# GNN and FFN layer on one core: tile 0 in float32, row statistics by ScalarE, counts placed along the products

## What is computed

```python
h = gat_layer(layernorm(x), W1, att_src1, att_dst1, b1, src, dst, heads=8, out_ch=128, concat=True)
h = relu(h)
x = x + gat_layer(h, W2, att_src2, att_dst2, b2, src, dst, heads=1, out_ch=768, concat=True)
x = x + ffn(layernorm(x)[None])[0]
# in a gat_layer: h = x @ W.T; logits a_src[src] + a_dst[dst], leaky_relu 0.2,
# softmax over the edges of one dst, out = sum of alpha * h[src]
```

## Time and profile before

| | us |
|---|---|
| median of 3 runs (lowest, highest) | 758.25 (758.07, 758.85) |
| profiled execution, its own time | 758.19 |
| its span, first to last instruction | 756.4 |
| PE busy in the span | 719.8 (95%) |
| DVE, ACT, POOL busy | 541.2, 370.2, 77.4 |

### The profile page before, as it was taken

How to read it: one execution, slowest core, us unless ns; L and a number is a source line. 1 busy time by engine, 2 the same in 40 slices (tenths; PEclk the granted TensorE clock), 3 DMA queues, 4 the chain that set the end, 5 groups by cost and what they waited for, 6 DMA issues and landing times.

```text
span 756.4 us, 12941 instructions
## 1 busy us (share of the span) xinstructions
PE 719.8 (95%) x4567; PEld 658.0 (87%) x4567; DVE 541.2 (72%) x983; ACT 370.2 (49%) x698; POOL 77.4 (10%) x94
## 2 busy tenths in 40 slices
PE   1879999988999999999999999999999999999988
PEld 1769999867899999999999999999988898888965
...
GB/s 298 132 89 174 156 188 152 168 180 282 97 46 57 102 34 69 34 68 47 54 200 0 1 55 0 1 0 34 220 278 76 179 106 165 90 70 168 21 27 56
DMA packets 39772, 78.97 MB, mean 104 GB/s; under 512 B 4057, under 2 KB 25500, under 8 KB 38829
## 3 DMA queue, kind: packets, MB, share of 16 engines
q1 hardware_dynamic: 34057, 60.60, 26.6%
...
## 4 chain that ended last, share of the span: by engine, by line
PE 88%; DVE 6%; ACT 3%; issue 2%; DVEq 1%; POOL 0%; DMA 0%; SPq 0%; ACTq 0%; POOLq 0%
PE bank L1104 22%; PE bank L1244 13%; PE bank L1085 12%; PE bank L1173 11%; PE bank L1017 11%; PE bank L1319 5%; PE bank L1339 4%; PE bank L943 2%; PE bank L1225 1%; PE bank L1120 1%; DVE y L1826 1%; PE bank L958 1%; PE bank L1291 1%; ACT w_hi L706 1%; PE bank L1307 1%
## 5 line engine op out<-in xcount | busy, mean ns | idle before, releaser
L1104 PE MATMUL bank<-PT,h1s 125*128 125x250 f32 x800 | 175.8, 374 | 0.0
L1104 PEld LDWEIGHTS bank<-PT,h1s 125*128 125x128 f32 x800 | 148.6, 190 | 15.6
L1658 DVE SCALAR_TENSOR_TENSOR L<-asb,nadh 125x1250 f32<-125x1250 f32 x80 | 118.0, 1517 | 6.7 <-PE bank L1085 4.8
L747 ACT COPY PT<-bank 125x500 f32<-125x500 f32 x200 | 100.1, 596 | 40.1 <-PE bank L1085 40.1
L1666 DVE CUSTOM_DVE_ANT_0 L<-L,LC 125x1250 f32<-125x1250 f32 x80 | 113.4, 1456 | 0.0
L734 ACT ACTIVATE L<-L,nm 125x1250 f32<-125x1250 f32 x80 | 107.7, 1370 | 2.1 <-DVE nm L1670 2.1
L1085 PEld LDWEIGHTS bank<-ident,L 125*125 125x125 f32 x800 | 95.4, 192 | 7.6 <-ACT L L734 4.8
L1085 PE MATMUL bank<-ident,L 125*125 125x125 f32 x800 | 96.5, 277 | 4.9 <-ACT L L734 4.6
L1836 DVE TENSOR_TENSOR x2f<-bank,x2f 125x384 f32<-125x384 f32 x20 | 10.3, 551 | 58.6 <-PE bank L1339 58.6
L1503 DVE TENSOR_TENSOR hotr<-iota,r 125x1500 f16<-125x1500 f16 x50 | 46.8, 935 | 3.1 <-issue 3.1
L1017 PE MATMUL bank<-w_hi,xT_hi 128*125 128x352 f32 (+2 forms) x168 | 37.1, 371 | 8.2 <-ACT w_hi L706 4.1
...
## 6 DMA issues: line engine op xcount, KB each, us to landing
...
```

Of the source, the lines that this page charges most:

```text
L747: act.copy(PT[(k - lag) % 2][:, 2 * b:2 * b + 2, :], bank[TBANK[b]][0:NP, 0:2 * GW].rearrange("p (s n) -> p s n", s=2)).then_inc(tb_evac, 1)
L1104: mm = pe.matmul(bank[2 + (k - lag) % 2][:, 0:GW], h1s[q][:, s, :], PT[(k - lag) % 2][:, s, :], start=(s == 0), stop=(s == NT - 1))
L1658: dve.scalar_tensor_tensor(L[r][:, :], asb[q][0:NP, 1, :], nadh[q][:, t:t + 1], asb[q][0:NP, 0, :], ALU.add, ALU.max).then_inc(stt_done, 1)
```

## The change

Tile 0 is multiplied in float32 by 18 matmuls straight from w1_sb (first_products), as soon as W1 comes, now in three transfers instead of two; its logits come from six small matmuls with watt1 (first_columns, read by DVE in first_column_out). Tile 1 takes over tile 0's former place. For tiles 2 to 9 ACT sums the rows and the squared differences with its accumulator (sums, squares) and POOL makes mean, variance, rstd and offset of them. ACT copies the 16 logit columns (cols) in features_out, in place of DVE's asc. Counts 2, 3, 4, 6, 7 and 8 stand between pieces of the products, 1 after tile 1's, 5 ahead of tile 5's, 9 ahead of turn(9). Products wait for each bank's copy (h1_piece) instead of all. 46 transposes of the identity, whose result is not used, stand ahead of and between PE's first steps. statistics(0) comes earlier on DVE, the ACT table load ahead of the loads of W1.

```diff
+            def scale_by_sums(t):
+                p = t % 2
+                pool.wait_ge(sum_ready, t - 1)
+                pool.tensor_scalar(stats[p][:, 0, 0:1], mv[p][:, 0:1], -1.0 / D, None, ALU.mult).then_inc(mean_ready, 1)
+                pool.wait_ge(sq_ready, t - 1)
+                pool.tensor_scalar(var[p][:, :], mv[p][:, 1:2], 1.0 / D, LN_EPS, ALU.mult, ALU.add).then_inc(rstd_ready, 1)
+                pool.wait_ge(rstd_ready, 2 * t - 1)
+                pool.wait_ge(xn_ready, t - 1)
+                pool.tensor_tensor(rstd[p][:, :], var[p][:, :], powers[:, 0:1], ALU.pow).then_inc(rstd_ready, 1)
+                pool.wait_ge(rstd_ready, 2 * t)
+                pool.wait_ge(mean_ready, t - 1)
+                pool.tensor_scalar(nmr[p][:, :], stats[p][:, 0, 0:1], rstd[p][:, 0:1], None, ALU.mult).then_inc(nmr_ready, 1)
             pool.wait_ge(powers_set, 2)
-            for t in range(NT):
-                scale_of(t)
+            scale_of(0)
+            scale_of(1)
+            for t in range(2, NT):
+                scale_by_sums(t)
...
-            for k in range(0, KD, 3):
-                act.dma_start(w1_sb[:, k:k + 3, 0:HC], W1T.rearrange("(k p) n -> p k n", p=128)[:, k:k + 3, :]
-                              ).then_inc(w1_in[k // 3], 16)
+            for k in range(0, KD, 2):
+                act.dma_start(w1_sb[:, k:k + 2, 0:HC], W1T.rearrange("(k p) n -> p k n", p=128)[:, k:k + 2, :]
+                              ).then_inc(w1_in[k // 2], 16)
...
-                for b, c0, c1 in (THIRDS if t < FUSED else HALVES):
+                pieces = THIRDS if t < FUSED else HALVES
+                for b, c0, c1 in pieces:
                     c1 = min(c1, HC)
                     c = act.copy(h1st[t % 2][:, c0:c1], bank[b][0:NP, 0:c1 - c0])
+                    if c0 != pieces[-1][1]:
+                        c.then_inc(h1_piece, 1)
+                if 0 < t < FUSED:
+                    freed(act, rows_full, t - 1)
+                    freed(act, col_done, t - 1)
+                    c = act.copy(cols[t % 2][:, :], bank[5][0:NP, LOGIT0:LOGIT0 + 2 * H])
                 c.then_inc(h1_out, 1)
+            def sums(t):
+                act.wait_ge(x_in[t % 2], TWO * (t // 2 + 1))
+                act.wait_ge(xt_full, t - 1)
+                act.activation(xn[t % 2][:, :], xin[t % 2][:, :], ACT.Identity, bias=0.0, scale=1.0,
+                               accum_out=mv[t % 2][:, 0:1]).then_inc(sum_ready, 1)
+            def squares(t):
+                act.wait_ge(mean_ready, t - 1)
+                act.activation(xn[t % 2][:, :], xin[t % 2][:, :], ACT.Square, bias=stats[t % 2][:, 0, 0:1], scale=1.0,
+                               accum_out=mv[t % 2][:, 1:2]).then_inc(sq_ready, 1)
...
-            rows_turned(0)
+            first_turned()
             for k in range(KD):
-                if k % 3 == 0:
-                    act.wait_ge(w1_in[k // 3], 16)
+                act.wait_ge(w1_in[k // 2], 16)
                 act.copy(w1_hi[:, k, 0:HC], w1_sb[:, k, 0:HC]).then_inc(w1_hi_done, 1)
             normalise(1)
+            sums(2)
+            squares(2)
+            features_out(0)
             rows_turned(1)
             log_counts(0)
             normalise(2)
-            log_counts(1)
-            features_out(0)
+            store_h1(0)
             load_x(4)
-            for i in range(1, NT):
-                if i > 1:
-                    features_out(i - 1)
-                    if i + 3 < NT:
-                        load_x(i + 3)
-                if i + 1 < NT:
-                    log_counts(i + 1)
-                store_h1(i - 1)
+            sums(3)
+            rows_turned(2)
+            squares(3)
+            normalise(3)
+            for i in range(2, NT):
+                features_out(i - 1)
+                if i in (2, 5, 8):
+                    log_counts({2: 1, 5: 5, 8: 9}[i])
                 if i + 1 < NT:
                     rows_turned(i + 1)
+                if i in (4, 7):
+                    log_counts({4: 4, 7: 8}[i])
+                if i + 3 < NT:
+                    load_x(i + 3)
                 if i + 2 < NT:
+                    sums(i + 2)
+                store_h1(i - 1)
+                if i + 2 < NT:
+                    squares(i + 2)
                     normalise(i + 2)
+                if i in (2, 3, 5, 6):
+                    log_counts({2: 2, 3: 3, 5: 6, 6: 7}[i])
...
+            def keep_busy(count):
+                for _ in range(count):
+                    pe.transpose(bank[3][:, 0:128], ident[:, :], ident[:, :])
             def spans_turned():
                 pe.wait_ge(consts_made, 2)
+                keep_busy(26)
                 pe.wait_ge(span_step, 6)
                 pe.transpose(bank[2][0:2 * NW, 0:NS], vv[:, :], ident[0:NS, 0:NS]).then_inc(span_turned, 1)
+                keep_busy(8)
                 pe.wait_ge(span_step, 7)
                 pe.transpose(bank[2][0:1, 128:128 + 2 * NW], vm[:, :], ident[0:2 * NW, 0:2 * NW]
...
+                        if part == 0 and b == 6:
+                            pe.wait_ge(h1_piece, 2 * t - 1)
+                        elif part == 0 and b == 7 and t < NT - 1:
+                            pe.wait_ge(h1_piece, 2 * t)
+                        elif part == 0:
+                            pe.wait_ge(h1_out, t)
                         for k in range(KD):
-                            if t == 0 and b == 6 and part < 2:
+                            if t == 1 and b == 6 and part < 2:
                                 pe.wait_ge((w1_hi_done, w1_lo_done)[part], k + 1)
...
+                        if count and (part, b) == count[0]:
+                            count_edges(count[1])
...
+            def first_products():
+                pe.wait_ge(xT_ready, 1)
+                for k in range(KD):
+                    pe.wait_ge(w1_in[k // 2], 16)
+                    for b, c0, c1 in THIRDS:
+                        c1 = min(c1, HC)
+                        mm = pe.matmul(bank[b][0:NP, 0:c1 - c0], xT_first[:, k, :], w1_sb[:, k, c0:c1],
+                                       start=(k == 0), stop=(k == KD - 1))
+                    mm.then_inc(w1_used if k < KD - 1 else h1_full, 1)
+            def first_columns():
+                pe.wait_ge(watt_done, 3)
+                for k in range(KD):
+                    mm = pe.matmul(bank[5][0:NP, LOGIT0:LOGIT0 + 2 * H], xT_first[:, k, :], watt1[:, k, :],
+                                   start=(k == 0), stop=(k == KD - 1))
+                mm.then_inc(first_logits, 1)
             spans_turned()
+            keep_busy(12)
             turn(0)
-            pe.wait_ge(xT_ready, 1)
-            products(0, parts=(0,), pieces=THIRDS[:2])
+            first_products()
+            turn(1)
             pe.wait_ge(consts_made, 14)
             pe.wait_ge(plan_ready, 1)
             count_edges(0)
-            turn(1)
-            products(0, parts=(1, 2), pieces=THIRDS[:2])
             pe.wait_ge(w1n_in, 16)
             pe.wait_ge(attz_set, 3)
+            pe.wait_ge(h1_out, 1)
...
-            count_edges(1)
+            products(1, parts=(0,), pieces=THIRDS[:2])
             pe.wait_ge(watt_done, 1)
...
-            pe.wait_ge(watt_done, 3)
-            products(0, pieces=THIRDS[2:])
-            count_edges(2)
-            for i in range(1, NT):
+            products(1, parts=(1,), pieces=THIRDS[:2])
+            first_columns()
+            turn(2)
+            products(1, parts=(2,), pieces=THIRDS[:2])
+            products(1, pieces=THIRDS[2:])
+            count_edges(1)
+            inside = {2: ((2, 6), 2), 3: ((1, 7), 3), 4: ((0, 7), 4), 5: ((2, 6), 6), 6: ((1, 7), 7), 7: ((0, 7), 8)}
+            for i in range(2, NT):
+                if i == 5:
+                    count_edges(5)
                 if i == NT - 2:
                     logit_products(i)
+                    count_edges(NT - 1)
                 if i < NT - 1:
                     turn(i + 1)
-                products(i)
-                if i + 2 < NT:
-                    count_edges(i + 2)
+                products(i, count=inside.get(i))
...
-            for k in range(KD):
-                dve.wait_ge(w1_hi_done, k + 1)
-                dve.tensor_tensor(w1_lo[:, k, 0:HC], w1_sb[:, k, 0:HC], w1_hi[:, k, 0:HC].bitcast(F32),
-                                  ALU.subtract).then_inc(w1_lo_done, 1)
-            rows_lower(0)
             dve.wait_ge(attz_set, 1)
             dve.wait_ge(att1_in, 16 * 2)
...
-            ahead = one_hots(1, *ahead)
-            statistics(2)
+            for k in range(KD):
+                dve.wait_ge(w1_hi_done, k + 1)
+                if k < KD - 1:
+                    dve.wait_ge(w1_used, k + 1)
+                else:
+                    dve.wait_ge(h1_full, 1)
+                dve.tensor_tensor(w1_lo[:, k, 0:HC], w1_sb[:, k, 0:HC], w1_hi[:, k, 0:HC].bitcast(F32),
+                                  ALU.subtract).then_inc(w1_lo_done, 1)
```

(45 more changed lines are left out.)

73 lines of the change are left out of this document (43 added, 30 removed).

## The result

The changed kernel takes 761.97 us (median of 7 runs, 760.2 to 763.12), the kernel before 758.24 in the same job (7 runs): a ratio of 1.0049, 95% interval [1.0036, 1.0063]. It is slower by 3.7 us, where 743.1 was predicted. The profiled execution took 762.04 us, its span is 760.2 (before: 756.4).

A forecast was written before the change was run, and what follows sets the result against it. DVE was taken to bound the entry and PE everything from about 60 us on, so only the entry's time could be won. 17.2 - 1.2 - 1.4 + 0.5 = 15.1 us off 758.2 gave 743.1 us, range 738.5 to 751.

The forecast's parts named there:

- The entry: Start-up before PE is saturated: earlier wrow1 copies and reordered DVE work were to win 17.2 us.
- turn(3): Transposes of tile 3, the fixed point for the shift: start at 45.6 us instead of 68.84, two counts still owed.
- the price of a POOL step behind DVE: Extra wait of each of POOL's four statistics steps a tile among DVE's one-hot compares: 0.7 us, bounds 0 and 1.13.
- two rows: Profile rows before the change: POOL's power at 54.06 and offset at 55.85, each 1.13 us longer beside DVE work.
- The 1.2 us: Predicted loss over seven tiles from ACT waiting for POOL's late statistics steps, beyond a slack of 2.7 a tile.
- shut out for a whole loop: POOL gets in only at the end of a 6.54 us one-hot loop: 48 us lost, 791; chance 0.07.
- Statistics off DVE: Tiles 2 to 9: frees about 1.4 us of DVE a tile, no gain here, but lets late one-hots keep up.
- Counts inside the products: Counts placed between PE's products: the same 3.02 us each, the same weight loads, no effect of their own.
- Tile 8: Logit_products(8) waits for tile 7's copies out of PSUM, which count(9) no longer hides: loss 1.4 us.
- Tile 9: Starts after one of two PSUM copies, not both, where PE waited 1.16 us: gain 0.5 us.
- Fillers: The 46 transposes ahead of and between PE's first steps: no gain, a faster clock being hidden by DVE's chain.
- The sum: All gains and losses together: 15.1 us off 758.2, giving 743.1 us.

The follow-up runs named there:

- e6: Changed kernel with mean, variance and offset of the statistics by ACT, so POOL has only the power, one step a tile; 757.59 us.
- e11: e6 plus one standstill of DVE a tile, behind the third group of one-hots; 749.88 us.
- e8_bench: Separate kernel, no reference work: one small POOL step released at the start of twelve back-to-back DVE instructions of one kind; each came through behind one DVE instruction.
- e16_bench3: Separate kernel, no reference work: one small POOL step released at different points of long DVE streams; 0.75 us in the first loop, 18.82 ahead of the second.
- e3: Changed kernel with statistics of tiles 2 to 9 by DVE again, power and offset by POOL, no sums or squares on ACT; 760.07 us.
- e5: Changed kernel with counts 2, 3, 4, 6, 7 and 8 behind a tile's products instead of between their parts; 770.69 us.
- e15: e11 with counts 2, 3, 4, 6, 7 and 8 behind their tile's products; 759.85 us.
- e10: Changed kernel with e6's ACT steps and two DVE standstills a tile, without the 46 filler transposes; 752.61 us, against 752.19 with them.
- e14: e11 with tile 9's counts ahead of tile 8's logit products again; 748.62 us.

## Why the prediction was wrong

- *The entry.* Right in kind, 1.7 us short. The wrow1 copies end at 34.2 where 33.8 was forecast, but the one-hots of tile 1 begin at 39.58, not 38.4, behind PE's products for the first columns and 0.63 us in which DVE waited for nothing that the profile shows, and turn(3) stands at 47.34, not 45.6: 15.5 us won for 17.2.
- **The failed step** is the price of a POOL step behind DVE: "Bounds: 0 and 1.13 for each. I take 0.7". Tile 4's mean waited 13.7 us (13.86 for 0.2), and cost 10.6 us with the cold restart. With ACT doing the other steps (4.4 us, e6) and one standstill a tile (7.7, e11) it is 749.9 for 762.0. I had read two rows in which a step waited for one DVE instruction, and took them for the nature of the wait. The rows are read rightly, and DVE didn't pause there either; but there is a second state of DVE, in which a step waits for its next standstill, and two rows couldn't bound that. The 1.2 us don't follow from the 0.7 even so: 4 x 0.7 - 2.7 = 0.1 a tile is 0.7 us over seven.
- *The rival "shut out for a whole loop"* had the mechanism, with a chance of 0.07, and my ground against it was one row of the state in which steps come through. Its size was wrong the other way: of the long holds (5.74 us in tile 2, 13.86 in tile 4) only tile 4's made PE wait, so 762 and not 791. By the Trainium skill (SBUF — State Buffer, the two separate sides) a DVE operation that has two SBUF inputs gets the shared ports for the whole of its instruction, and a GpSimd operation is blocked meanwhile. The page doesn't say that the next DVE instruction gets them again. e8_bench agrees with one instruction as the wait (0.74 to 1.36 us); as a bound, which is what I made of it, e16_bench3 contradicts it, with 18.82 us. The measurement decides.
- *Statistics off DVE are "no gain, what lets the late one-hots keep up".* No gain by itself, as said. It isn't what took the pause away, either: with the statistics on DVE again (e3) POOL is held for 9.78 to 17.71 us. The pause before was DVE's wait for ACT's h1st ahead of the column copy (0.73 us), which in the new order DVE doesn't meet; no run puts that back by itself. DVE had 10.17 us to spare right behind the stream, and used none of it earlier.
- *Counts inside the products, "nothing of its own"*: wrong both ways. The counts take 3.0 us more in the changed kernel, of which moving them back regains 1.1 to 1.6, and the placing saves 9 to 10 net (e5, e15) by covering ACT. I had priced ACT's two passes, but not what they stand in front of.
- *Tile 8*, 1.4 us predicted: 2.28 and 1.2 for the low clock. *Tile 9*: 0.77 us of wait for 1.16, 0.4 gained for 0.5. *Fillers*: nothing (e10), as predicted.
- *The sum.* The miss is 18.9 us. Entry 1.7, tile 4 10.6, counts 3.0, tile 8 2.1 make 17.4 of it, less the 1.2 that I had allowed for; some 2.7 us are spread over short waits that I didn't trace. e14, with POOL's wait and tile 8's wait for the columns gone, is at 748.6, 5.5 above the forecast: the counts again (28.6 us for 25.4) and turn(3) at 48.39 (2.8) are as large as that together.

Open: why some counts are slow, between products and behind them. In count 4 PE steps at 0.61 to 0.71 us a round, in count 5 at 0.56 to 0.60; I found no single wait that goes with it, and tried nothing for it.
